# Cross attention: the exponential of two of four units made from PSUM head by head, with the negated maximum as its bias

## The reference

```python
Q = split_heads(query @ Wq.T + bq)          # 16 heads of 16 columns
K = split_heads(key @ Wk.T + bk)            # 77 rows of context
V = split_heads(value @ Wv.T + bv)
scores = einsum('bhqd,bhkd->bhqk', Q, K) / scale
scores = where(mask == 0, -1e10, scores)
attn = softmax(scores, axis=-1)             # over the 77 rows
h = einsum('bhqk,bhkd->bhqd', attn, V)
x = x + h @ Wo.T + bo
```

## Time and profile before

| | |
|---|---|
| median of 3 runs | 628.3 us (625.84 to 629.01) |
| profiled execution | 627.66 us, of which the span of the trace 625.9 us |
| busy, whole span | PE 560.3, DVE 462.0, ACT 338.2, POOL 263.4 us |
| cross attention | units from 24.6 us to about 134 us of the span |

### The profile page before, as it was taken

The page is one execution under the profiler, slowest core; times in us unless marked ns, Lnnn a source line. Parts: engine busy times, 40 slices in busy tenths (PEclk is TensorE's granted clock), DMA queues, the critical chain, the costliest instruction groups (busy, mean ns, idle before and its releaser), DMA issues. The chain is left out here.

```text
span 625.9 us, 11700 instructions
## 1 busy us (share of the span) xinstructions
PE 560.3 (90%) x3620; PEld 495.7 (79%) x3620; DVE 462.0 (74%) x925; ACT 338.2 (54%) x615; POOL 263.4 (42%) x288
## 2 busy tenths in 40 slices
PE   3779999995899999999999999899747999999993
PEld 3669998984588888888888888666746999999993
DVE  4798999994227888888888898496664775785672
ACT  3345656543247887877877887034303642662351
POOL 4145545670014443444434453114426682683311
PEclk9779999998889999999999999897757999999997
DMA  8245422200422222322223300631416671571110
GB/s 253 52 113 137 125 81 50 51 1 1 114 47 68 51 52 64 83 57 52 51 57 71 76 1 2 233 142 68 136 25 220 210 286 42 207 253 43 34 30 0
DMA packets 25401, 56.99 MB, mean 91 GB/s; under 512 B 5112, under 2 KB 9977, under 8 KB 23304
## 3 DMA queue, kind: packets, MB, share of 16 engines
q1 hardware_dynamic: 21608, 48.80, 26.5%
q0 software_dynamic: 2256, 5.55, 3.0%
q10 hardware_dynamic: 1488, 2.05, 1.1%
HBM read 33.28 MB, written 4.87 MB: 61 GB/s over the span
## 5 line engine op out<-in xcount | busy, mean ns | idle before, releaser
L974 POOL TENSOR_SCALAR h_p<-h_p,h_rs 128x1024 f32<-128x1024 f32 x64 | 72.4, 1131 | 116.1 <-DVE h_rs L1069 116.1
L1076 DVE TENSOR_REDUCE h_nmx<-h_psS 128x1 f32<-128x1024 f32 x64 | 78.1, 1221 | 28.7 <-PE h_psS L1155 27.3
L998 ACT CAST h_pTh<-h_psT 128x512 fp32r<-128x512 f32 x128 | 69.2, 590 | 31.3 <-PE h_psT L1113 31.2
L1056 DVE TENSOR_TENSOR h_pTl<-h_psT,h_pTh 128x512 fp32r<-128x512 f32 x128 | 81.4, 677 | 4.5 <-ACT h_pTh L998 4.5
L1025 ACT ACTIVATE h_p<-h_psS,h_nmx 128x1024 f32<-128x1024 f32 x64 | 72.3, 1129 | 14.0 <-DVE h_nmx L1076 14.0
L1124 PE MATMUL h_psO<-h_pTh,h_vs 128*128 128x256 f32 x256 | 69.9, 306 | 3.0 <-DVE oT L1064 2.2
L1113 PE MATMUL h_psT<-ident,h_p 128*128 128x128 f32 x512 | 67.5, 273 | 1.4 <-DVE h_pTl L1056 1.2
L1113 PEld LDWEIGHTS h_psT<-ident,h_p 128*128 128x128 f32 x512 | 59.3, 141 | 11.4 <-issue 3.3
L1124 PE MATMUL h_psO<-h_pTl,h_vs 128*128 128x256 f32 x256 | 63.6, 282 | 0.0
L371 POOL TENSOR_TENSOR a_p<-a_p,a_rs 128x616 f32<-128x616 f32 x32 | 38.9, 1217 | 57.6 <-DVE a_rs L477 57.6
L1155 PE MATMUL h_psS<-h_kh,h_qs 128*128 128x512 f32 x128 | 55.7, 435 | 0.0
(11 more groups left out here) (316 smaller groups left out, 1405.2 us busy)
## 6 DMA issues: line engine op xcount, KB each, us to landing
wst<-in_m_w SPq DMA_DIRECT2D x16, 1024.0 KB, 6.3
bias<-in_m_b SPq DMA_DIRECT2D x8, 640.0 KB, 6.8
h_kh<-h_hi SPq DMA_DIRECT2D x30, 128.0 KB, 2.4
h_kl<-h_lo SPq DMA_DIRECT2D x30, 128.0 KB, 2.3
fw<-in_f_w SPq DMA_DIRECT2D x8, 384.0 KB, 3.9
rows<-x_all SPq DMA_DIRECT2D x4, 518.0 KB, 3.5
a_qs<-a_qhi SPq DMA_DIRECT2D x16, 128.0 KB, 2.3
a_qf<-a_qhi SPq DMA_DIRECT2D x16, 128.0 KB, 2.4
```

Of the source, the lines that this page charges most:

```text
L974: pool.tensor_scalar(pr[:, u % 4], pr[:, u % 4], rs[:, u:u + 1], 0.0, ALU.mult, ALU.add).then_inc(pn_ready, 1)
L998: act.copy(pTh[u // QP % 2][:, hf * HK:(hf + 1) * HK, u % QP * P:(u % QP + 1) * P], psT[hf][:]).then_inc(pT_hi, 1)
L1056: vec.tensor_tensor(pTl[u // QP % 2][part], psT[hf][:], pTh[u // QP % 2][part], ALU.subtract).then_inc(pT_lo, 1)
L1076: vec.tensor_reduce(nmx[:, u:u + 1], psS[u % 2][:], AX.X, ALU.max, negate=True).then_inc(max_ready, 1)
```

## The change

BY_HEAD = (1, 3) names two of the four units of each tile. In these units DVE computes the negated maximum and no subtraction, and counts sub_done after the maximum. ACT makes the exponential from PSUM (psS) instead of from pr, in eight instructions of 77 columns, one for each head, with the head's negated maximum as bias, and writes pr. PE's scores of unit u + 2 wait for exp_done where unit u is one of the two, as ACT still reads psS then. The guard that pr's transposes are done moves from DVE to ACT. per_pair counts fewer links.

```diff
+        BY_HEAD = (1, 3)
@@ ACT, body
                     upto(act, sub_done, i, 2 * U, g + 1)
-                    act.activation(pr[:, u, 0:HL], pr[:, u, 0:HL], ACT.Exp).then_inc(exp_done, 1)
+                    if u in BY_HEAD:
+                        upto(act, pT_ps, i, 2 * U, g + 1 - U)
+                        for head in range(HH):
+                            a, j = divmod(head, GH)
+                            ins = act.activation(pr[:, u, head * L:(head + 1) * L], psS[u % KD][:, a, j * L:(j + 1) * L],
+                                                 ACT.Exp, bias=mx[:, u, head:head + 1], scale=1.0)
+                    else:
+                        ins = act.activation(pr[:, u, 0:HL], pr[:, u, 0:HL], ACT.Exp)
+                    ins.then_inc(exp_done, 1)
@@ DVE, body
                     upto(vec, s_ps, i, 2 * U, g + 1)
-                    link(vec.tensor_reduce(mx[:, u].rearrange("p (a g) -> p a g", a=2), s4, AX.X, ALU.max))
-                    upto(vec, pT_ps, i, 2 * U, g + 1 - U)
-                    vec.tensor_tensor(pr[:, u, 0:HL].rearrange("p (a g l) -> p a g l", a=2, g=GH), s4,
-                                      mx[:, u].rearrange("p (a g) -> p a g", a=2).unsqueeze(3)
-                                      .to_broadcast([P, 2, GH, L]), ALU.subtract).then_inc(sub_done, 1)
+                    most = mx[:, u].rearrange("p (a g) -> p a g", a=2)
+                    if u in BY_HEAD:
+                        vec.tensor_reduce(most, s4, AX.X, ALU.max, negate=True).then_inc(sub_done, 1)
+                    else:
+                        link(vec.tensor_reduce(most, s4, AX.X, ALU.max))
+                        upto(vec, pT_ps, i, 2 * U, g + 1 - U)
+                        vec.tensor_tensor(pr[:, u, 0:HL].rearrange("p (a g l) -> p a g l", a=2, g=GH), s4,
+                                          most.unsqueeze(3).to_broadcast([P, 2, GH, L]),
+                                          ALU.subtract).then_inc(sub_done, 1)
-            per_pair = 2 * (2 * U) + 2 * 2
+            per_pair = 2 * (2 * U - len(BY_HEAD)) + 2 * 2
@@ PE, body
-                    upto(pe, sub_done, i, 2 * U, g - 1)
+                    upto(pe, exp_done if (g - 2) % U in BY_HEAD else sub_done, i, 2 * U, g - 1)
```

## The result

| | before | after |
|---|---|---|
| median | 628.2 us (6 runs, 624.8 to 631.2) | 622.7 us (6 runs, 621.5 to 623.9) |
| ratio after / before | | 0.9921, 95% interval 0.9896 to 0.9947 |
| profiled execution, span | 627.66 us, 625.9 us | 622.69 us, 620.9 us |

A forecast was written before the change was run, and what follows sets the result against it. DVE was taken as the bound, with PE 4% behind. Gains of 1.0 (start), 1.8 (four full tiles), 0.4 (tile 6) and 0.6 us (end) sum to 3.8 us, from 628.3 to 624.5 us; range 621.5 to 628.8.

The forecast's parts named there:

- DVE is the bound, PE 4% behind: Cross-attention, full tiles: DVE sets the 13.76 us period; removing 1.60 us a tile puts it under PE.
- PE's floor: Full tiles: PE's own work plus its wait before the query, 13.17 us a tile, limiting the gain to 2.4 us.
- The sum: Gains of start 1.0, four full tiles 1.8, tile 6 0.4 and the end 0.6: 3.8 us.
- Eight heads in 1.9 us: ACT in units 1 and 3: eight 77-column exponentials take 1.9 us in place of one of 0.72 us.
- the line through L1025 and L222 and the pair: ACT pricing from two measured exponentials and two L222 in a row: 0.31 us alone, one every 0.22 us, eight 1.85.
- The chain through the copy of h is just hidden: Unit 3: exponential, then copies of x and h before PE's next query; hidden with some 0.1 us to spare.
- the edge: Unit 3's exponential: from 2.0 us on, each 0.1 us more costs 0.1 us a tile.
- The start: Tiles 0 and 1: gain between 0.35 and 1.6 us, taken as 1.0 us.
- The tail: Tile 6 gains 0.4 us; tile 7 and the end 0.6 us, despite the last unit's longer exponential.
- "Faster" at 52%: Whole kernel: 52% chance of a measured gain beyond 0.5% (3.1 us); same 42%, slower 6%.
- more at the start: Rival, tiles 0 and 1: shorter waits keep PE's clock up, up to 2 us more gained, 622.5 us; 15%.
- The rival with a gain taken back: Unit 3: eight heads cost 2.3 us, the copy of h delays queries, 1.5 us gained, 626.8 us; 26%.

The follow-up runs named there:

- e3_keep_sub: The change, but DVE still makes a subtraction of 616 columns in units 1 and 3 into an unread tile; ratio 1.0037 against the kernel before.
- e1_unit1: The change in unit 1 alone, with unit 3 as before; ratio 0.9937 against the kernel before.
- e4_one_exp: The change, but one exponential of 616 columns from PSUM in units 1 and 3, without the maximum as bias; ratio 0.9920 against the kernel before.
- e5: The change with two more exponentials of 77 columns in unit 3, ten for eight; ratio 0.9964 against the kernel before.
- e6: The change with four more exponentials of 77 columns in unit 3 (e6_four_more); ratio 1.001 against the kernel before.
- e9_pool_early: The change, with POOL making the router's constants of units 1 to 3 in tile 0 instead of tile 6; ratio 0.9924 against the kernel before.
- e11_unit1_pool: The change in unit 1 alone, with POOL's router constants made in tile 0; ratio 0.9932 against the kernel before.
- e2_unit3: The change in unit 3 alone, with unit 1 as before; ratio 0.9993 against the kernel before.

## Why the prediction was right, and where it was off

- **DVE is the bound, PE 4% behind.** Right, and shown by putting the work back (e3_keep_sub). PE's floor was read as 13.17 us a tile; 13.16 was measured, with PE busy for 99% of it.
- **The sum.** 3.8 us were forecast for the change, and the profiles tie 3.5 to it. That this is so close is in part luck, as two errors cancel: the full tiles gave 0.6 us more than forecast, and tile 6 to the gate 0.7 us less.
- **Eight heads in 1.9 us.** 1.84 measured, 1.85 by the line through L1025 and L222 and the pair. The rule of the Trainium skill ("ScalarE: Activation LUTs", section "What ACT_TABLE_LOAD costs") gave 2.1 us for the eight. One instruction of 77 columns took 346 ns, close to the rule's 344 and above the line's 310; the spacing is 0.21 us ((1.84 - 0.35) / 7) against the rule's 0.25. So the trace agrees with its price of one instruction, and successive ones overlap by more, 0.13 us instead of 0.09.
- **The chain through the copy of h is just hidden.** Right in mechanism, off in size: I added 0.1 us of stall a tile for a late DVE, which is not there, and put the edge at 2.0 us, where it is at about 2.15. The stall that was not there is why the four tiles gave 2.40 us in place of 1.8 (a period of 13.16 against 13.3); the edge cost nothing, as the 1.84 us lie under both.
- **The start.** 1.0 forecast, 0.87 measured. The wait of the query for the copy of x was named: 0.35 us of gain were expected there, and the query came 0.50 us earlier after unit 1 of tile 0 (10.84 us in place of 11.34). e1_unit1 and e4_one_exp, without the eight instructions in unit 3, start 0.8 to 0.9 us faster still, but with a clock of 1.00 in tile 1. At that clock e5 and e6 take 22.58 and 23.01 us with ten and twelve exponentials, so eight would take about 22.15 us (an estimate from these two). Most of the 0.8 to 0.9 us then goes with the clock, and 0.1 to 0.2 with the exponential.
- **The tail.** This step failed: 0.4 + 0.6 us forecast, 0.26 measured. Tile 6 gave its part (0.53 us); I had taken the longer last exponential as mostly covered, and tile 7 lost 0.57. The rows of the kernel after, of DVE, ACT and POOL:

```profile
127.07 1.84 ACT L281 ACTIVATE a_p<-a_psS,a_mx 128x77 f32<-128x77 f32 x8
...
128.94 0.80 DVE L485 TENSOR_REDUCE a_sm<-a_p 128x8 f32<-128x616 f32 x1 [1.50 <-ACT a_p L281]
...
130.06 1.27 POOL L380 TENSOR_TENSOR a_p<-a_p,a_rs 128x616 f32<-128x616 f32 x1 [0.45 <-DVE a_rs L486]
```

  The last sums wait 1.50 us for the last exponential, and POOL's last scaling 0.45 us for them. Cut the tail at the end of this scaling: it comes 26.77 us after the start of tile 6, and 26.81 before, so POOL gained nothing. The rest takes 22.02 us, and 22.24 before. The dose runs show the same path: with two and four more exponentials the scaling ends at 27.24 and 28.10 us, and the rest stays at 22.02 and 22.03; e9_pool_early has 25.95 and 22.02. Yet without the long exponential the tail is no shorter. In e1_unit1 and e4_one_exp the scaling ends at 26.65 and 26.21 us, but the rest takes 22.80 and 22.79. DVE's normalisation then runs longer beside POOL's last scalings: the four of it take 2.97 and 3.16 us in place of 2.23, and 1.38 us later on, where POOL is idle. Whether this alone makes the rest longer is open: e11_unit1_pool has 2.23 us there and a rest of 22.48.
- **Chances.** "Faster" at 52% came out. The medians say 5.5 us and the ratio 5.0, of which the profiles tie 3.5 to the change. The median of 622.7 us lies by the 622.5 of the rival "more at the start", but not by its mechanism: the mean clock of tiles 0 and 1 was 0.82 against 0.81, and the start gave 0.87 us. The rival with a gain taken back did not come, and e6_four_more shows its price where it does.

## What to carry to other kernels

When one engine is the bound by 4% over the next, removing 12% from it (1.60 us of a tile of 13.76) buys 4%; half of the edit (unit 1 alone) bought the same here, and which half is told by what waits behind the longer instruction, not by the sum of busy time. Follow each lengthened instruction to the copies queued behind it and give the chain a margin in microseconds: here 0.30 us, after which each 0.1 us of exponential cost 0.1 us a tile. Small changes are better judged by stretches of the profile between marks around the edit, which repeated to 0.1 us in two executions, than by whole times, which ran over 2 to 10 us for one program. But read the granted clock of each stretch first: in the start it changed by as much as the effects that were looked for.

## What the runs showed of the hardware

Before the first instruction that differs, the two profiles are already 1.10 us apart. TensorE's granted clock explains it. The clock falls to half after the same pause in both, but between 22 and 23 us before and only between 24 and 25 us after. The windows from 20 to 28 us show it, first of the kernel before and then of the one after (columns as above):

```profile
20.00:28.00 8.00, 6.08 (x28) 5.41 (x27) 5.59 (x10) 1.30 (x2) 0.00 (x0) 0.63 0.29 66
```

```profile
20.00:28.00 8.00, 6.07 (x31) 5.19 (x30) 6.24 (x14) 1.30 (x2) 0.00 (x0) 0.79 0.29 68
```

The first scores start at 23.14 and 23.15 us, after 1.92 us of waiting for a DMA in both, but the first of them takes 0.59 us at the lower level (1.2 GHz) in one and 0.39 us at the full 2.4 GHz in the other. Between 400 and 470 us the mean clock was 0.81 in e2_unit3 and 0.69 in e9_pool_early, and the part after the gate took 464.3 and 473.8 us, with the same instructions. Over 23 executions of the kernel before on one chip, the time falls as the mean clock rises, from 631.42 us at 0.939 to 624.19 us at 0.950 (correlation -0.89). How soon and how often the clock falls differs from execution to execution, and that goes with most of the spread that one program shows here; no run holds the clock fixed.
